# A four-layer graph network kernel: in the second convolution, the bias halves of gathered rows move to ScalarE and a block's gathers are issued in three parts

## The reference, cut to what matters

```
h = relu(layernorm(x))
w = (relu(edge_attr_6 @ W1 + b1) @ W2 + b2).reshape(E, 16, 16)    # a 16x16 matrix per edge
msg = einsum('ei,eio->eo', h[src], w)                             # per edge
agg = segment_sum(msg, dst) / max(deg, 1) + bias
x = x + batchnorm(relu(agg))
```

## Time and profile before

| | |
|---|---|
| median of 3 runs | 9811.56 us (9802.76 to 9813.1) |
| span of the profiled execution | 12237.7 us |
| second layer's walk within that span | about 1675 to 4464 us |
| GpSimd busy over the span | 6721.1 us (55%) |
| TensorE busy | 8203.0 us (67%) |
| VectorE busy | 7355.8 us (60%) |
| ScalarE busy | 4559.7 us (37%) |

### The profile page before, as it was taken

One profiled execution on the slowest core, in us unless ns is written; L12 is line 12 of the kernel. 1 busy time (PEld: TensorE's weight loads), 2 busy tenths in 40 slices (PEclk: granted clock), 3 DMA queues, 4 the chain that ended last, 5 costly groups with the idle time before them and its releaser, 6 DMA issues. The chain is left out here.

```text
span 12237.7 us, 134310 instructions
## 1 busy us (share of the span) xinstructions
PE 8203.0 (67%) x35152; PEld 4483.7 (37%) x35152; DVE 7355.8 (60%) x11821; ACT 4559.7 (37%) x7372; POOL 6721.1 (55%) x6397
## 2 busy tenths in 40 slices
PE   4777735666666633666665656666568888888885
PEld 3555623333333322333333333333323333333332
DVE  5555523444444443555555545555479889888888
ACT  4555533444444412333333333334223232333333
POOL 6776744333333345444444444444377777777775
PEclk8878756666666656777777777777779999999997
DMA  3111110111111110000101000010112222222223
GB/s 124 48 47 51 45 28 23 25 25 25 25 25 25 25 19 17 19 19 17 20 17 19 19 17 19 17 19 14 15 56 75 69 75 69 75 71 73 72 73 93
DMA packets 498922, 493.18 MB, mean 40 GB/s; under 512 B 180303, under 2 KB 396134, under 8 KB 497959
## 3 DMA queue, kind: packets, MB, share of 16 engines
q1 hardware_dynamic: 298823, 371.60, 9.0%
q0 software_dynamic: 199904, 119.78, 6.5%
HBM read 240.96 MB, written 249.95 MB: 40 GB/s over the span
## 5 line engine op out<-in xcount | busy, mean ns | idle before, releaser
L1915 POOL DMA_INDIRECT sheaf_got<-tab,sheaf_idx x1612 | 1649.1, 1023 | 2106.4 <-DVEq L2314 1631.8
L2454 POOL DMA_INDIRECT attn_got<-tab,attn_line x1760 | 2094.0, 1190 | 723.5 <-issue 517.5
L2003 PE MATMUL sheaf_acc<-sheaf_hot_hi,sheaf_wide 128*128 128x392 bf16 x6696 | 1544.8, 369 | 869.7 <-issue 700.3
L2507 PE MATMUL attn_q<-attn_X,ident 128*128 128x512 f32 x3520 | 1810.6, 661 | 1.8 <-DVE attn_X L2679 1.8
L1673 DVE TENSOR_TENSOR nnconv_prod<-nnconv_w,nnconv_got 128x1024 f32<-128x1024 f32 x434 | 491.7, 1145 | 1375.8 <-remote 1035.5
L1451 POOL DMA_INDIRECT nnconv_got<-tab,nnconv_idx x1116 | 1055.8, 946 | 370.1 <-issue 321.2
L2003 PEld LDWEIGHTS sheaf_acc<-sheaf_hot_hi,sheaf_wide 128*128 128x128 bf16 x6696 | 695.5, 112 | 1530.6 <-issue 1254.6
L2206 DVE TENSOR_SCALAR sheaf_hot_hi<-sheaf_number,src_hi 128x784 bf16<-128x784 f16 x1116 | 467.4, 419 | 1304.9 <-remote 1135.6
L2640 DVE TENSOR_TENSOR attn_T<-attn_w,attn_got 128x1024 f32<-128x1024 f32 x880 | 1035.4, 1218 | 285.4 <-issue 208.3
L1166 POOL DMA_INDIRECT gcn_got<-tab,gcn_idx x868 | 976.4, 1125 | 305.9 <-issue 271.4
L2507 PEld LDWEIGHTS attn_q<-attn_X,ident 128*128 128x128 f32 x3520 | 702.7, 211 | 1141.0 <-issue 1141.0
(11 more groups left out here) (501 smaller groups left out, 15154.4 us busy)
## 6 DMA issues: line engine op xcount, KB each, us to landing
sums<-attn_S SPq DMA_DIRECT2D x110, 1024.0 KB
tops<-attn_S SPq DMA_DIRECT2D x110, 512.0 KB
attn_got<-tab,attn_line POOLq DMA_INDIRECT x1760
sheaf_got<-tab,sheaf_idx POOLq DMA_INDIRECT x1612
gcn_key<-src_key SPq DMA_DIRECT2D x62, 384.0 KB
gcn_blk<-src_blk SPq DMA_DIRECT2D x62, 384.0 KB
nnconv_got<-tab,nnconv_idx POOLq DMA_INDIRECT x1116
nnconv_key<-src_key SPq DMA_DIRECT2D x62, 256.0 KB
```

The source lines that it names most:

```text
L1915: e.indirect_dma_start(out=got[at.b][:, j, D:D + T2], out_offset=None, in_=tab[2], in_offset=indices(idx[at.b], j)).then_inc(s_got[j // JH ...
L2003: mm = e.matmul(pacc[k][:, 0:HH], wide[at.b][half][:, part, col, :], hot[:, k * HH:(k + 1) * HH], start=False, stop=False, skip_group_chec ...
L2454: e.indirect_dma_start(out=got[at.b][:, 4 * q + n, :], out_offset=None, in_=tab[3], in_offset=indices(ids[:, q, n, :], D + 2)).then_inc(s_ ...
L2507: e.matmul(to, ident[:, :], X[:, q, :, n, :], start=n == 0, stop=False)
```

## The change

Four things change in the second layer.

1. ScalarE gets a new step, `biased`: it copies the bias halves of a block's 26 columns out of `got` into a new tile `bias_part` (128 partitions x 16 x 26 numbers), after it has waited for all the block's rows. It stands between `stored` and `flagged`, for the block before.
2. VectorE's add at the end of a block reads `bias_part` in place of `got`.
3. GpSimd no longer waits for `s_run` of the block two back. It waits for `s_bias` of that block, copies the indices, and issues the gathers as 8, 8 and 2 columns. Before each part it waits until VectorE's products of the block two back have read these columns: groups 0 and 1, groups 2 and 3, group 4.
4. Each part has semaphores of its own. VectorE waits for a part ahead of the first product that reads it (groups 0, 2 and 4), and for ScalarE's 8 columns from group 4 on.

```
+            PARTS = ((0, 8, 1), (8, 16, 3), (16, JN, 4))
+            part_of = [next(n for n, (_, _, last) in enumerate(PARTS) if g <= last) for g in range(PARTS[-1][2] + 1)]
+            bias_part = sbl("bias_part", [P, D, J])
...
                     def gather(at):
                         if at.k >= 2:
-                            e.wait_ge(s_run[at.b], at.half(1, 0))
+                            turn_wait(e, s_bias, at.of(1, -1))
                         e.tensor_copy(idx[at.b][:, :], srci[:, bass.ds(at.of(J, 0), JN)]).then_inc(s_idx, 1)
                         turn_wait(e, s_idx, at.of(1, 1))
-                        for j in range(JN):
-                            e.indirect_dma_start(out=got[at.b][:, j, :], out_offset=None, in_=tab[1],
-                                                 in_offset=indices(idx[at.b], j)).then_inc(s_got[at.b], 16)
+                        for part, (j0, j1, last) in enumerate(PARTS):
+                            if at.k >= 2:
+                                turn_wait(e, s_msg, at.of(NG, last + 3 - 2 * NG))
+                            for j in range(j0, j1):
+                                e.indirect_dma_start(out=got[at.b][:, j, :], out_offset=None, in_=tab[1],
+                                                     in_offset=indices(idx[at.b], j)).then_inc(s_got_of[part][at.b], 16)
...
+                    def biased(at):
+                        for part, (j0, j1, _) in enumerate(PARTS):
+                            e.wait_ge(s_got_of[part][at.b], at.half(16 * (j1 - j0), 16 * (j1 - j0)))
+                        e.wait_ge(s_moved, at.of(GN, GN + 2))
+                        e.copy(bias_part[:, :, :], by_feature(got[at.b][:, :, D:])).then_inc(s_bias, 1)
+
                     def step(at):
                         more = at.k < NB - 1
                         if at.k >= 2:
                             stored(at.plus(-2))
+                        biased(at.plus(-1))
                         flagged(at)
...
-                        if g == 0:
-                            e.wait_ge(s_got[at.b], at.half(16 * JN, 16 * JN))
+                        if g < len(part_of) and (g == 0 or part_of[g] > part_of[g - 1]):
+                            j0, j1, _ = PARTS[part_of[g]]
+                            e.wait_ge(s_got_of[part_of[g]][at.b], at.half(16 * (j1 - j0), 16 * (j1 - j0)))
+                        if 4 * g + n > JN:
                             e.wait_ge(s_moved, at.of(GN, GN + 2))
...
-                        ch.to(e.tensor_tensor(msgT[at.b][:, :, 1:], msgT[at.b][:, :, 1:], by_feature(got[at.b][:, :, D:]), ALU.add))
+                        e.wait_ge(s_bias, at.of(1, 1))
+                        ch.to(e.tensor_tensor(msgT[at.b][:, :, 1:], msgT[at.b][:, :, 1:], bias_part[:, :, :], ALU.add))
```

More of the change, by code:

```diff
@@ L1391, in gnn_kernel @@
             s_t, s_edge = (seml(f"{n}_even", f"{n}_odd") for n in ("t", "edge"))
-            s_ef, s_rows, s_got, s_run, s_st, s_kept = (
-                seml(f"{n}0", f"{n}1") for n in ("ef", "rows", "got", "run", "st", "kept"))
+            s_ef, s_rows, s_got_a, s_got_b, s_got, s_run, s_st, s_kept = (
+                seml(f"{n}0", f"{n}1") for n in ("ef", "rows", "got_a", "got_b", "got", "run", "st", "kept"))
+            s_got_of = (s_got_a, s_got_b, s_got)
+            s_bias, = seml("bias")
             run_rows = runs[1].rearrange("(p l) f -> p l f", p=P)
@@ L1626, in _ @@
                     step(At(NB - 1))
-                    for k in (NB - 2, NB - 1):
-                        stored(At(k))
+                    stored(At(NB - 2))
+                    biased(At(NB - 1))
+                    stored(At(NB - 1))
                 @block.vector
```

## The result

The changed kernel takes 9743.3 us (median of 3 runs, 9732.96 to 9748.4) against 9811.56 (9802.76 to 9813.1): ratio 0.993, 95% interval 0.9912 to 0.9948, some 68 us faster. The forecast was 9798, a change of 13 us. The time lies inside the range, but the gain is five times the forecast one.

A forecast was written before the change was run, and what follows sets the result against it. The prediction took ScalarE's and SyncE's cycle to bound a second-layer block in timed runs, with gathers having slack. It summed -10 us (add) and -3 us (DMA) to -13 us, from 9811.6 to 9798 us, range 9710 to 9890.

The forecast's parts named there:

- Gathers have slack: Second layer: gathers land 2.4 to 9 us before they are needed, so starting them earlier gains 0.
- rival 2: Gathers bound timed runs if a block is under 24.8 us; up to 2 us a block gained, 9690 us; chance 0.17.
- ScalarE's copy: New copy of bias halves, 0.98 us a block, hidden by ScalarE's later waits for loads: cost 0.
- Rival 4: ScalarE's copy isn't covered by waits, so its 0.98 us a block counts: 9860 us; chance 0.07.
- VectorE's add: Add at a block's end falls from 0.92 to 0.593 us; half of 0.33 us counted, 10 us in all.
- DMA traffic: SyncE's write no longer meets the first gathers; 0.05 us a block taken, 3 us in all.
- Remote waits: ScalarE's and VectorE's long waits for TensorE's signals, 10.2 us of ScalarE's profiled block, are largely absent from timed runs.
- signals queue behind TensorE's records: Inferred origin of those waits: TensorE's signals seem held behind its profile records while GpSimd's gather burst runs.
- Rival 3: TensorE's signals are held up in timed runs too; split gathers lengthen blocks 1.1 to 3 us, about 9880 us; chance 0.19.
- The sum, -13 us: Second layer: 10 us from the add and 3 us from DMA traffic, all other terms 0, giving 9798 us.
- Faster would say that gathers were waited for.: Sign for timed runs: a move of more than 0.4% to faster would mean that gathers were waited for.
- the forecast's own range: Whole kernel: 9765 to 9830 us for no or little change, forecast 9798; chance 0.57.

The follow-up runs named there:

- e1_copy_only: The changed kernel with all 18 gathers in a row after the scan, as before the change; ScalarE's copy and the new add stay: 9749.99 us, ratio 0.9925.
- e3_dense_add: The kernel before, its add reading an unstrided tile of zeros; bias halves left out of the result, no ScalarE copy: 9743.1 us, ratio 0.9922.
- e8_delay_in_loop: The kernel before with one idle memset ahead of the second layer and a 700-column memset each turn of VectorE's third-layer loop: 9767.6 us, ratio 0.9946.
- e11_32_more: The kernel before with 32 small idle memsets more on VectorE, third-layer loop after 1287 instructions: 9753.56 us, ratio 0.9931.
- e4_one_more: The kernel before with one single-column memset that nothing reads, in VectorE's prologue of the second layer: 9743.02 us, ratio 0.9929.
- e2_one_part: The changed kernel with its 18 gathers as one part, started after the fifth product of the block two back: 9747.92 us, ratio 0.992.

## Why the prediction was right and wrong

- **Gathers have slack: 0.** Right. `e1_copy_only`, without early gathers, is as fast as the change within the measurement, and no first product waits for a gather in either profile. A block takes 1930.6 / 61 = 31.6 us (forecast 29.4 to 33.7), longer than the 24.8 below which rival 2 would have decided.
- **ScalarE's copy: 0, covered.** Right. It takes 0.92 us (forecast 0.98), and ScalarE's wait ahead of `moved` shrinks from 107.6 to 73.1 us in the stretch, 0.7 us a block; in every profile with the copy it is 67 to 76 us, in every one without it 103 to 112. Rival 4 did not come about.
- **VectorE's add: 0.16 us a block, 10 us in all.** The duration is right (0.59). Its worth isn't to be seen: `e3_dense_add`, which has it alone, takes 1932.0 us between scans against 1930.6.
- **DMA traffic: 3 us.** Within what the layer shows, not told apart. The whole edited layer gained 2.1 us for the forecast 13; but the same layer also varies between 1928.5 (`e8_delay_in_loop`) and 1933.3 us (`e11_32_more`) among kernels that leave its blocks alone, so no gain of it is shown.
- **Remote waits belong to the profiled execution.** Right: 9818.4 us without them. The forecast block was near, too (31.6 us). That signals queue behind TensorE's records was an inference and was not tested. Rival 3 lost its ground with the waits.
- **The sum, -13 us: the step that failed.** It summed over the edited layer alone and took the rest of the kernel as unmoved, because its code is. The missing term is the third layer, -64 us: the change added 19 VectorE instructions ahead of that layer's loop. They did no work there; they moved it off a place where it lost 3.0 us a turn (85.34 against 82.38). `e4_one_more` shows it with one instruction, and the kernels that begin the layer at the same moment with another count that no shift in time does it. Also the sum's -13 us in the edited layer is not shown: 2.1 us were measured there, less than the layer varies.
- **"Faster would say that gathers were waited for."** Wrong, by the same step: faster came from elsewhere.
- **The range, 9710 to 9890.** That 9743 lies in it is luck. It was made that wide for rivals 2 and 3, and neither came about; the forecast's own range began at 9765. The prediction said that it would be wrong if the timed runs moved by more than 0.4%, and they moved by 0.7%.

What of the 3.2 us is explained? By the waits 1.0 us is lost at the turn itself, some 0.65 of it behind the branch by the records. By hand 0.64 us there cost 1.0 us a turn (`e8_delay_in_loop`), so by proportion the loss may stand for a third of it (0.65 us) to a half (1.0 us). The rest isn't explained. It shows as longer waits of VectorE for ScalarE (174.7 against 109.0 us), which waits for TensorE, and goes with a granted clock of 0.90 and 0.91 in the two slow kernels against 0.94 and 0.95 in the others. The clock may be the cause, or what follows from more idle time; no run here tells that apart. That the two packets hinder each other is read from their order and durations at one position only, in two kernels; a second slow position, where another of the moving packets would fall just behind the branch, was not tried.

The Trainium skill (Runtime: NRT & Kernel Launch, "Instruction fetch mechanics") says that an engine fetches instructions in blocks ahead of itself, and that a taken branch to a block no longer held stalls until it has been fetched. The trace agrees in kind: 2.8 us or more from the branch to the next instruction with a body of 366 instructions. In the last layer, whose body has 134, hardly any packet moves. The page gives blocks of 16 KiB; the packets here have 8 KB, and for this kernel the measurement holds.

## What to carry over

Before an edit is credited with a gain, compare the layers that it didn't touch: here 64 of 72 us came from one of them. Where an engine runs a long loop, a control with one idle instruction ahead of it is cheap: if it is as fast as the edit, the gain is the place's. None of the kernels here beats the changed one beyond the measurement, and the kernel before with one idle memset equals it (9743.02 against 9743.3), so the change itself has shown no worth of its own.

## What the runs showed of the hardware that was not expected

- A loop of 366 VectorE instructions spends 2.8 us between its branch and the next instruction on each turn, and moves five instruction packets of 8 KB. The loops of the other layers, of 85 to 134 instructions, spend 0.2 to 0.3 us there (medians, second profile of the kernel before) and move none in most turns.
- Where such a loop starts in the program decides 2.8 to 3.4 us of an 82 us turn: 1255 instructions ahead of it gave 85.3, seven other counts from 1256 to 1319 gave 82.0 to 82.5 (83.0 with the delay of `e8_delay_in_loop`).
- Between fast positions there is still a difference of up to 17 us (2484.8 us for the third layer in `e2_one_part`, 2502.2 in the changed kernel), of which nothing is explained.
- One profiled execution in two of the same kernel was 2419 us longer than the other (12237.7 and 9818.4 us), with the same instructions and with remote waits in it. A block of the second layer took 43.9 us in the one and 31.6 in the other.
